# A hint for the loop-closing branch on every engine: a state-space layer between two ternary feed-forward layers

## The reference

```python
x = x + 0.5 * ffn(layernorm(x), W_up, W_gate, W_down)   # weights ternary: clip(round(W/scale), -1, 1) * scale
x = x + attn(layernorm(x), ...)                         # a selective state-space layer, 1024 channels, 16 states
x = x + 0.5 * ffn(layernorm(x), W_up, W_gate, W_down)
# inside attn, per token l:  h = h * exp(delta * A) + (delta * x) * B_l ;  y_l = sum over states of h * C_l
# then (y + x * W_D) * silu(skip), times W_out
```

## Time and profile before

| | us |
|---|---|
| median of 3 runs (lowest, highest) | 3110.82 (3110.68, 3111.58) |
| time of the profiled execution | 3112.23 |
| its span, first to last instruction | 3110.4 |
| PE busy in the span | 2812.5 (90%) |
| DVE busy | 2704.1 (87%) |
| POOL busy | 1999.7 (64%) |
| ACT busy | 1814.3 (58%) |
| mean granted TensorE clock | 0.957 |

### The profile page before, as it was taken

One profiled execution on the slowest core, in us unless ns is written; L12 is line 12 of the kernel. 1 busy time (PEld: TensorE's weight loads), 2 busy tenths in 40 slices (PEclk: granted clock), 3 DMA queues, 4 the chain that ended last, 5 costly groups with the idle time before them and its releaser, 6 DMA issues.

```text
span 3110.4 us, 59394 instructions
## 1 busy us (share of the span) xinstructions
PE 2812.5 (90%) x18791; PEld 2212.6 (71%) x18791; DVE 2704.1 (87%) x3613; ACT 1814.3 (58%) x4212; POOL 1999.7 (64%) x1875
## 2 busy tenths in 40 slices
PE   4777899989999998999999999999999999999778
PEld 3556677777867777786777778677776877777655
DVE  6359998989989898998989899898988989899993
ACT  6265656565665656566565655656565565656551
POOL 2165766757666675766767576676757667675761
PEclk8888899999999999999999999999999999999898
DMA  6010001001010100101010010101001010100100
GB/s 246 28 32 21 32 18 39 21 23 35 18 36 21 39 19 22 39 18 36 21 36 21 23 39 18 36 21 36 18 21 41 16 39 21 35 19 21 35 28 7
DMA packets 53402, 100.87 MB, mean 32 GB/s; under 512 B 7805, under 2 KB 9145, under 8 KB 52537
## 3 DMA queue, kind: packets, MB, share of 16 engines
q1 hardware_dynamic: 53048, 96.45, 9.5%
HBM read 87.78 MB, written 8.65 MB: 31 GB/s over the span
## 4 chain that ended last, share of the span: by engine, by line
PE 70%; DVE 14%; issue 8%; ACT 2%; DVEq 1%; POOL 0%; ACTq 0%; POOLq 0%
PE ps L1415 19%; PE ps L1426 14%; PE ps L1377 12%; PE ps L1438 11%; PE ps L1491 7%; DVE h L1164 6%; DVE y L1190 3%; PE ps L1464 2%; PE ps L1447 2%; PE ps L1454 2%; DVE xc L1233 2%; PE ps L1399 1%; DVE xw L1256 1%; DVE act L1198 1%; PE ps L1482 1%
## 5 line engine op out<-in xcount | busy, mean ns | idle before, releaser
L647 POOL TENSOR_TENSOR h<-u,bb 128x1024 f32<-128x1024 f32 x512 | 1222.6, 2388 | 376.7 <-PE ps L1377 365.7
L880 ACT ACTIVATE ps<-delta,a_neg 128x255 f32<-128x255 f32 x2048 | 882.2, 466 | 669.9 <-DVE h L1164 669.4
L1164 DVE TENSOR_TENSOR_SCAN h<-ps,h 128x512 f32<-128x512 f32 x1024 | 1192.3, 1206 | 50.7 <-POOL h L651 42.9
L1190 DVE SCALAR_TENSOR_TENSOR y<-ps,ccur,y 128x512 f32<-128x512 f32 x960 | 671.0, 740 | 59.4 <-PE ps L1377 58.3
L1377 PE MATMUL ps<-ident,h 128*128 128x128 f32 x4096 | 557.4, 279 | 102.8 <-DVE y L1190 99.3
L1377 PEld LDWEIGHTS ps<-ident,h 128*128 128x128 f32 x4096 | 477.6, 143 | 175.0 <-issue 80.4
L1415 PE MATMUL ps<-xh,q_gate 128*128 128x256 f16 x2048 | 462.3, 273 | 38.9 <-DVE act L1198 22.6
L1415 PE MATMUL ps<-xh,q_up 128*128 128x256 f16 x2048 | 466.2, 274 | 6.2 <-DVE xl L1103 3.2
L1415 PE MATMUL ps<-xl,q_up 128*128 128x256 f16 x2048 | 465.7, 274 | 0.0
L1415 PE MATMUL ps<-xl,q_gate 128*128 128x256 f16 x2048 | 462.1, 273 | 0.0
L742 POOL TENSOR_TENSOR hl<-act,hh 128x512 f16<-128x512 f32 x256 | 301.3, 1179 | 220.8 <-ACT hh L905 220.8
(11 more groups left out here) (133 smaller groups left out, 3474.9 us busy)
## 6 DMA issues: line engine op xcount, KB each, us to landing
bb<-b_scratch SPq DMA_DIRECT2D x224, 256.0 KB, 3.1
xs<-in_L_attn_resid_dram SPq DMA_DIRECT2D x17, 512.0 KB, 3.4
out_dram<-xs SPq DMA_DIRECT2D x16, 512.0 KB, 3.9
wraw<-in_L_ffn_W_up_dram SPq DMA_DIRECT2D x4, 1024.0 KB, 8.8
wraw<-in_L_ffn_W_gate_dram SPq DMA_DIRECT2D x4, 1024.0 KB, 13.1
wraw<-in_L_ffn_W_down_dram SPq DMA_DIRECT2D x4, 1024.0 KB, 14.2
w_in<-in_L_attn_W_in_dram SPq DMA_DIRECT2D x1, 2048.0 KB, 21.5
w_skip<-in_L_attn_W_skip_dram SPq DMA_DIRECT2D x1, 2048.0 KB, 8.8
```

The costliest lines, as they stand in the source:

```text
L647: pl.tensor_tensor(h[:, s % RING, :, :], u[:, :, :], bb[:, planes_of(s) % 2, s % PLANES:s % PLANES + 1, :].broadcast_to([P, HE, CH]), ALU. ...
L880: ins = ac.activation(abar[r][:, e, 1:], delta[:, k, 1:], ACT.Exp, scale=a_neg[:, k, n:n + 1])
L1164: v.tensor_tensor_scan(hr, abar[r].rearrange("p e t -> p (e t)"), hr, 0.0, ALU.mult, ALU.add).then_inc(scanned, 1)
L1190: ins = v.scalar_tensor_tensor(out=yy, in0=hT[:, t, :], scalar=cc, in1=yy, op0=ALU.mult, op1=ALU.add)
```

## The change

The loop of each engine is opened through the program-wide form of the same loop, for that one engine, with `hint_back_edge=True`:

```diff
             run("fill", -1)
             run("first", 0)
-            with eng.Fori(1, NCH - 1) as i:
+            with nc.Fori(1, NCH - 1, engines=(eng.engine,), hint_back_edge=True) as i:
                 run("loop", i)
             run("last", NCH - 1)
             run("drain", NCH)
```

## The result

The changed kernel takes 3059.4 us (median of 4 runs, 3058.6 to 3060.0) where the kernel before takes 3110.8 (3110.0 to 3111.6): the ratio is 0.9835, with a 95% interval of 0.9818 to 0.9852. That is 51.3 us less; the forecast was 3057 and 54 us less. The profiled execution took 3058.6 us, its span is 3056.8, which is 53.6 less than the span of before.

The account below looks back on a forecast made before the run. It took PE's order of work as the bound, with PE standing still for an instruction fetch at each taken loop branch. Saving 55 us less 1 for the last turn gave 54, from 3110.8 to 3057 us, range 3044 to 3080.

Parts of the forecast that it names:

- PE's stall: At PE's taken loop branch, the 4.35 us fetch wait shrinks to about 0.1; 4.25 us in 13 turns saves 55 us.
- The check by turn 1: Turn 1, entered without a taken branch, took 178.25 us against 182.48 for later turns; 4.23 us times 13 is 55.0.
- The last turn: At the final fall-through the hint is wrong; a late fetch costs nothing to 4.6 us on PE, taken as 1.
- DVE's and ACT's misses: Behind the loop branch, DVE's 2.8 and ACT's 2.6 us a turn end too, counted at nothing because other waits cover them.
- DVE's place: From DVE's last y_add to its first L1198, there is room for 3.8 to 4.8 us saved a turn.
- The clock: PE's half-clock stretch behind the branch may go with the idle time: nothing in the forecast, at most 0.5 us a turn.
- the low end: The whole kernel at 3044 us, if all gaps and the half-clock stretches go.
- q8 and q14: Instruction queues per turn: q8 brings 11 packets in place of 12, and q14 falls by two or more.
- B: At the loop branch the hint does nothing and the stalls stay: 3110.8 to 3112 us, chance 8%.
- C: The stall moves one block behind the branch, 0.3 to 3.5 us a turn: 3060 to 3102 us, chance 7%.
- D: Fetch starts when the hint executes at the turn's top, displacing a needed block; a second stall, 3168 us, chance 5%.

Follow-up runs that it names:

- PE alone: The changed kernel with the hint kept in PE's loop only, none on the other engines: 3057.0 us, and 3059.2 us when timed again.
- the last experiment: The changed kernel with DVE's history mask L1219 moved from ahead of its slot's y_add to behind it: 3050.5 us, ratio 0.9807 to the kernel before.
- slot 30: The changed kernel with PE's hint moved from the turn's top to the start of slot 30, 9.2 us ahead of the branch: 3061.8 us.
- slots 16: The changed kernel with PE's hint moved from the turn's top to the start of slot 16, 95 us ahead of the branch: 3060.4 us.

## Why the prediction came out as it did

*PE's stall (55 us): right.* 54.95 us by the windows. The "issue" wait is 0.22 us a turn instead of 0.1, and the branch 0.36 us instead of about 0.1. What was off is the taken branch on PE, for which I took POOL's 0.2 us. The check by turn 1 (178.25 us) came within 0.01 us of the turn measured. It holds the leftovers of all engines, and so was a better number than the sum of parts. That it is so near is luck in part: the 178.26 is the mean of ten turns of about 177.9 us and three of 179.5 to 179.6, and in a second run of the same kernel, with two such turns, it was 178.11.

*The last turn (1 us): not borne out.* In the profile 1.5 us are lost behind the last branch, near what I took; but I had priced a late fetch on PE, and that fetch, 2.2 us behind the branch, costs PE no wait. It is DVE that shows a step, and without the step the time is the same. Kernels alike vary by 5 us in that stretch. Whether the wrong hint costs anything at the end stays open.

*DVE's and ACT's misses at nothing: right, for a wrong reason.* I wrote that POOL's L651 would hold DVE anyway. Without the miss the scan's wait fell from 1.96 us to 0.56, and the releaser was ACT. What makes it free is the next operation: L1219 isn't done before POOL's L647 ends, so it takes back the 1.2 us. The price in the sum was right; the sentence "had the misses stayed while PE's went, they would be the next thing in the way" is wrong, and PE alone shows it: 178.25 us a turn with them.

*DVE's place (3.8 to 4.8 us): right, near its lower end.* From its last y_add to L1198 it takes 877.56 - 865.30 = 12.26 us, 4.15 less than in the earlier trace rows. That row was one branch of 13, between 15.8 and 17.3 us; their mean went from 16.23 to 12.27 us, 3.96 less.

*The clock (nothing, at most 0.5 a turn): right in size.* T1's eight transposes take 1.09 us, full speed, behind seven of the 13 branches now, 1.96 or 1.97 as before behind three, and something between behind the other three. Around the branch after turn 2 the chain reads

```profile
688.03 1.97 PE ps L1399 x8
690.00 4.21 PE ps L1491 x8
694.20 0.87 PE ps L1377 x8
```

where PE ran in order of time behind the branch after turn 3

```profile
867.63 1.09 PE L1399 MATMUL ps<-ident,xn 128*128 128x128 f32 x8 [0.22 <-issue]
868.56 3.60 PE L1491 MATMUL ps<-w_out,gz 128*128 128x512 f32 x8
872.06 1.22 PE L1377 MATMUL ps<-ident,h 128*128 128x128 f32 x8
874.11 0.27 PE L1415 MATMUL ps<-xh,q_up 128*128 128x256 f16 x1 [0.82 <-DVE xl L1103]
```

PE is at L1377 again after 4.4 us instead of 6.2, but waits 0.82 us for DVE right behind it, and the chain of that turn goes over DVE with L1219 in it (869.52 to 871.11). So what the clock gives back there is lost in the wait for DVE, which stands in just those seven turns.

The reading that the fall comes from the stall's idle time is not borne out. Before, PE's last transposes end at 875.33 us, and the granted clock, still 1.00 up to 875.90, is 0.50 from there on, 0.6 us into the gap. And in the kernel of the last experiment, which has no stall, it falls behind all 13 branches, and T1 takes 1.68 to 1.97 us (windows of before and of that kernel, columns as in the earlier trace rows):

```profile
875.90:879.30 3.40, 0.00 (x0) 0.00 (x0) 2.90 (x4) 1.59 (x6) 2.94 (x4) 0.50 0.18 57
865.80:869.00 3.20, 3.20 (x10) 2.16 (x10) 3.20 (x5) 2.60 (x8) 2.77 (x3) 0.50 0.17 58
```

In both, as ahead of every branch, PE had waited 2.1 us for DVE before its last transposes. So the rule I cited from the Trainium skill ("TensorE: Matmul & The Clock Gate", Part 1), that idleness brings the throttle back, may well hold. What failed is that the slow stretch would go with the stall; the low end that I took from it wasn't reached. What decides in which turns the clock falls stays open.

*q8 and q14.* q8's eleven packets a turn were right. q14 fell by six a turn, "two or more": I had counted one block for each engine, but ACT's whole loop stays on the chip.

*The rivals.* B fell: the 13 demanded fetches are gone, and slot 30 shows a fetch that is neither the next nor demanded. The sentence beside B, that prefetch is purely sequential, is of the page "Runtime: NRT & Kernel Launch" of the Trainium skill (Instruction fetch mechanics); for a hinted branch it doesn't hold here, with 361 ns where there were 4576. What the same section says of a taken branch out of the held window, the kernel before bears out, with one q8 packet in the stall. C fell: the one gap a few us behind the branch, 0.6 to 0.8 us in seven turns, is PE's wait for DVE's L1103. D's premise fell with slots 16 and 30: a hint at the top starts nothing until PE is in the branch's block. D would have been right had the fetch started when the hint executes, and slot 30 shows that a hint given inside that block acts within about 2 us.

## What to carry to other kernels

Look at the duration of the loop's branch on every engine, one record a turn, and at the first turn against the rest: here the first gave the cause and the second the whole gain before anything was built. Only the engine that the chain goes through needed the hint. Given 9 us ahead of the branch or more it was in time, the turn's top being as good as any place; 0.2 us ahead was too late, and between the two nothing was tried. When a small operation lasts several times its usual length, compare its end with the ends of the other engines' work: L1219 looked busy and was waiting, and moving it was worth another 9 us, 5 of them through the clock in a way that isn't shown.

## What the runs showed of the hardware that was not expected

- A hint given 179 or 95 us ahead of the branch starts the fetch 15 us ahead of it; I read this as a hint that is kept until the block of the branch is reached. Given 9 us ahead, it starts a fetch about 2 us later, behind a sequential one that has already gone out (187 packets instead of 174). Given 0.2 us ahead it saves nothing (4555 ns).
- On ACT a loop of 374 instructions missed in each turn (2.6 us, five packets) or never, by where it began, with no hint (155 against 90 packets).
- After a hint that was wrong, PE fetched 2.2 us behind the branch and didn't wait for it; with the direction right no fetch came for 19.5 us.
- DVE's L1219, of 128x24 int32, lasted 0.18 us by itself and 0.21 to 1.84 beside POOL's L647, and ended 0.03 to 0.05 us behind it each time. The Trainium skill ("SBUF — State Buffer", Who interferes with whom) says that a DVE instruction with two inputs in SBUF contends with a GpSimd instruction that reads SBUF, and that the lock is exclusive; the trace agrees, and it shows the wait inside the busy time of the one that is held.
- PE's taken branch lasts 0.36 us with the hint. What it lasts without one when its target is there, no run shows. POOL's first register operation follows its branch by 0.27 us without a hint and 0.29 with one.
